# A cross-attention and FFN kernel: the token products first, the low-rank products second, those of the output weight behind the first quad

## The chip, the cores and the metric

One core of one Trainium2 chip. Times are device microseconds (us) of one execution. 1000 ns are 1 us. f32 is a 4-byte float; fp32r is the 4-byte form that TensorE multiplies in one pass; f32 takes it two.

## The reference

x is 64 sequences of 128 tokens, 256 wide. The context has 64 x 128 tokens of 192 channels; the last 4 of each sequence are separate context tokens with weights of their own.

```
q_in = xn @ Wq + xn @ q_down @ q_up * (alpha/32)          # xn = layernorm(x); Wq: 256 x 1024
k_in = org_ctx @ Wk + (the same with k_down, k_up)        # org_ctx: the first 124 tokens; Wk: 192 x 1024
v_in = org_ctx @ Wv + (the same with v_down, v_up)
out  = attention(q_in, k_in, v_in)                        # 16 heads of 64
out += attention(q_in, ipa_ctx @ Wk_ipa, ipa_ctx @ Wv_ipa)  # ipa_ctx: the last 4 tokens
x    = x + out @ Wo + bo + out @ o_down @ o_up * (alpha/32)
x    = x + ffn(layernorm(x))   # ternary weights w1, w2, a depthwise convolution over tokens, silu
```

The low-rank pairs have rank 32.

## The kernel before, in words

The five engines' instruction streams are written out by hand, each in one block (`block.sync`, `block.tensor`, `block.scalar`, `block.vector`, `block.gpsimd`), and wait for each other by semaphores. SP only issues transfers; so do ACT's first fourteen instructions. The work has two parts: a prologue that prepares the weights, and a loop over 16 groups of 4 sequences, in which each step of a group (`project`, `scores`, `p_v`, `finish` and the others) has a fixed place among 32 half steps, and steps of neighbouring groups are interleaved. The change touches the prologue alone.

In the prologue:

- `project(At(0), n)` for n below `EARLY_HALVES` = 10 loads x and the context of group 0, normalises x (POOL takes the power at L1008), transposes it (L394) and splits context and x into a high fp32r part (ACT, L606 to L611) and a low part (VectorE, L781 to L786).
- `lora_product(i)`, 12 times, multiplies down and up of a low-rank pair: 32 rows by 128 columns against 32 rows by 512, in f32, into one of five PSUM banks (L542). VectorE adds each product to the raw weight (a merge, L924). 4 products belong to Wq, 8 to Wk and Wv.
- Each raw weight of 128x1024 is then split: ACT writes the high part (`high_part`, L695), released by a count of merges (`du_of_split`), and VectorE the low part (`low_part`, L906). Numbers 0 and 1 are Wq's halves, 2 to 5 are WK, WV and the two remainders WKR and WVR, 6 and 7 the output weight's halves.
- The separate context tokens of all 64 sequences are multiplied by Wk_ipa (8 products of 2 matmuls with 96 rows and 256 columns, L558 and L559) and by Wv_ipa (4 products of 2 matmuls with 512 columns, L562 and L563). ACT copies the results (L704, L707), SP stores them to DRAM (L357, L358), from where each group loads its share; w1 and w2 are loaded into the same buffer when the stores have landed.
- `lora_product(i)` for i of 12 to 15 makes the output weight's low-rank product, 8 matmuls of 256 columns (L546), also with 32 rows.
- `project(At(0), n)` for n from 10 to 31 computes Q, K and V of three of the four quads of heads: for each quad two tiles of each, in the order Q0, K0, V0, Q1, K1, V1 (L405 six matmuls of 512 columns, L414 five, L424 ten of 256), which take turns in two PSUM banks. `N_V[1]` = 16 is the place of the first quad's V1. ACT copies Q (two copies into QM, L617 and L618), K (L623) and V1, VectorE copies V0 (L791).

The raw weights lie in buffers that the loop uses later: Wq, Wk and Wv and two of the up weights in QM, v_up and o_down in KT, the down weights in X2, the output weight in GBS, the token weights in V. So nothing may be copied to QM or KT before all raw weights in QM have been split; TensorE, ACT and POOL wait for that (`w_low`). POOL then zeroes half of QM (L1038, L1040), since each head pair is kept twice with one head's rows zero, and copies the token columns into KT (L1015).

The loads: SP issues x, context, Wq, Wk, Wv, the token weights and tokens, and Wo, in this order; ACT issues the alphas and the low-rank operands on its own queue.

Of the kernel before, what the change touches and what calls it, by code (L numbers as in the profile page):

```python
# [20 lines left out]
F32 = mybir.dt.float32  # L21
F32R = mybir.dt.float32r
BF16 = mybir.dt.bfloat16
ALU = mybir.AluOpType
# [3 lines left out]
P = 128  # L28
SEQS, TOK, DM = 64, 128, 256
CD = 192  # L30
CH = CD // 2
HEADS, DH = 16, 64
ID = HEADS * DH
RANK = 32
# [6 lines left out]
PAIRS = HEADS // 2  # L41
QUADS = HEADS // 4
CHUNKS = QUADS * NB
HALVES = 2 * CHUNKS
# [11 lines left out]
N_XT = 8  # L56
# [3 lines left out]
N_Q, N_K, N_V = (10, 14), (11, 15), (13, 16)  # L60
# [5 lines left out]
EARLY_HALVES = N_XT + 2  # L66
# [69 lines left out]
def program(nc, x, ctxT, cipaT, Wq, Wk, Wv, Wo, bo, q_downT, q_up, k_downT, k_up, v_downT, v_up, o_downT, o_up,  # L136
            alphas, Wk_ipa, Wv_ipa, w1T, conv_w, conv_b, w2T, out):
    with ExitStack() as ctx:
# [3 lines left out]
        def sem(name):  # L142
            return ctx.enter_context(nc.semaphore(name))
# [10 lines left out]
        BO = sb("BO", [P, DM])  # L154
# [66 lines left out]
        small_in = [sem(f"small_in{i}") for i in range(3)]  # L221
        w_in = [sem(f"w_in{i}") for i in range(5)]
        du_full, du_used = sem("du_full"), sem("du_used")
        wsum, wsum_all, wscale = sem("wsum"), sem("wsum_all"), sem("wscale")
        w_high, w_low = sem("w_high"), sem("w_low")
        wq_steps = sem("wq_steps")
# [71 lines left out]
        splits += [(wo_raw[:, 4 * k:4 * k + 4, :], WO[0][:, 4 * k:4 * k + 4, :], WO[1][:, 4 * k:4 * k + 4, :], 1.0) for k in range(2)]  # L298
        du_of_split = [2, 4, 7, 8, 11, 12, 14, 16]

        block = ctx.enter_context(nc.Block())
# [3 lines left out]
        def _(sp):  # L305
# [36 lines left out]

            for n in range(EARLY_HALVES):
                project(At(0), n)

            sp.dma_start(wq_raw, Wq.rearrange("(k p) n -> p k n", p=P)).then_inc(w_in[0], 16)
            for t, tr, src in ((wk_raw, wkr_raw, Wk), (wv_raw, wvr_raw, Wv)):
                sp.dma_start(t, src[0:P, :]).then_inc(w_in[1], 16)
                sp.dma_start(tr[0:64, :], src[P:CD, :]).then_inc(w_in[1], 16)
                sp.dma_start(tr[64:128, :], src[P:CD, :]).then_inc(w_in[1], 16)  # L350
            for t, tr, src in ((wki_raw, wkir_raw, Wk_ipa), (ci_t, cir_t, cipaT), (wvi_raw, wvir_raw, Wv_ipa)):
                sp.dma_start(t[0:CH, :], src[0:CH, :]).then_inc(w_in[4], 16)
                sp.dma_start(tr[0:CH, :], src[CH:CD, :]).then_inc(w_in[4], 16)
            sp.dma_start(wo_raw, Wo.rearrange("(k p) n -> p k n", p=P)).then_inc(w_in[2], 16)

            sp.wait_ge(kv_used, 12)
# [24 lines left out]
        def _(pe):  # L381
# [145 lines left out]
            pe.wait_ge(ident, 3)  # L527
            for n in range(EARLY_HALVES):
                project(At(0), n)

            def lora_product(i):
                need(pe, du_used, i - 4)
                if i == 0:
                    pe.wait_ge(small_in[0], 3 * 16)
                if i == 4:
                    pe.wait_ge(small_in[1], 6 * 16)
                if i == DU_O:
                    pe.wait_ge(small_in[2], 5 * 16)
                bank = PS[:, i % 5, :]
                if i < DU_O:  # L540
                    dn, k, up, c, _, _ = du[i]
                    mm(bank, dn[0:RANK, P * k:P * k + P], up[0:RANK, 512 * c:512 * c + 512], start=True, stop=True).then_inc(du_full, 1)  # L542
                else:
                    for a in range(2):
                        k = 2 * (i - DU_O) + a
                        m = mm(bank[:, DM * a:DM * a + DM], o_dn_t[0:RANK, P * k:P * k + P], o_up_t[0:RANK, :], start=True, stop=True)  # L546
                    m.then_inc(du_full, 1)

            for i in range(DU_O):
                lora_product(i)  # L550

            pe.wait_ge(w_in[4], 6 * 16)
            pe.wait_ge(du_used, DU_O)
            for i in range(12):
                need(pe, kv_used, i - 2)
                bank = PS[:, i % 3, :]
                if i < PAIRS:
                    mm(bank[:, 0:256], wki_raw[0:CH, P * i:P * i + P], ci_t[0:CH, :], start=True, stop=False)  # L558
                    mm(bank[:, 0:256], wkir_raw[0:CH, P * i:P * i + P], cir_t[0:CH, :], start=False, stop=True).then_inc(kv_full, 1)  # L559
                else:  # L560
                    a, c = divmod(i - PAIRS, 2)
                    mm(bank, ci_t[0:CH, P * a:P * a + P], wvi_raw[0:CH, 512 * c:512 * c + 512], start=True, stop=False)  # L562
                    mm(bank, cir_t[0:CH, P * a:P * a + P], wvir_raw[0:CH, 512 * c:512 * c + 512], start=False, stop=True).then_inc(kv_full, 1)  # L563
            pe.wait_ge(kv_used, 12)
            for i in range(DU_O, DU_N):
                lora_product(i)
            pe.wait_ge(w_low, 6)
            for n in range(EARLY_HALVES, HALVES):
                project(At(0), n)
            pe.wait_ge(zeroed, 2)  # L570
            pe.wait_ge(w_low, len(splits))

# [28 lines left out]
        def _(act):  # L601
# [76 lines left out]

            for t, src in ((SMALL[:, 0:4], alphas.broadcast_to([P, 4])), (q_dn_t[0:RANK, :], q_downT), (q_up_t[0:RANK, :], q_up)):
                act.dma_start(t, src).then_inc(small_in[0], 16)  # L680
            for t, src in ((k_dn_t[0:RANK, 0:CD], k_downT), (v_dn_t[0:RANK, 0:CD], v_downT),
                           (k_dn_t[0:RANK, CD:256], k_downT[:, P:CD]), (v_dn_t[0:RANK, CD:256], v_downT[:, P:CD]),
                           (k_up_t[0:RANK, :], k_up), (v_up_t[0:RANK, :], v_up)):
                act.dma_start(t, src).then_inc(small_in[1], 16)
            for t, src in ((o_dn_t[0:RANK, :], o_downT), (o_up_t[0:RANK, :], o_up),
                           (BO[:], bo.broadcast_to([P, DM])), (CW[:], conv_w), (CB[:], conv_b)):
                act.dma_start(t, src).then_inc(small_in[2], 16)
            for n in range(EARLY_HALVES):
                project(At(0), n)

            def high_part(i):

                raw, high, _, factor = splits[i]
                act.wait_ge(du_used, du_of_split[i])
                act.activation(high, raw, ACT.Identity, scale=factor).then_inc(w_high, 1)  # L695

            for i in range(6):
                high_part(i)

            for i in range(12):  # L700
                act.wait_ge(kv_full, i + 1)
                bank = PS[:, i % 3, :]
                if i < PAIRS:
                    act.activation(ki_all[:, :, i, :], bank[:, 0:256].rearrange("p (g n) -> p g n", g=GROUPS), ACT.Identity).then_inc(kv_used, 1)  # L704
                else:
                    a, c = divmod(i - PAIRS, 2)
                    act.activation(vi_t[:, a, 512 * c:512 * c + 512], bank, ACT.Identity).then_inc(kv_used, 1)  # L707
            for i in range(6, len(splits)):
                high_part(i)
            act.wait_ge(w_low, 6)  # L710
            act.wait_ge(du_used, DU_N)
            for n in range(EARLY_HALVES, HALVES):
                project(At(0), n)
            act.wait_ge(small_in[2], 5 * 16)

# [19 lines left out]
        def _(dve):  # L735
# [164 lines left out]
            dve.wait_ge(w_in[0], 16)  # L900
            low = 0

# [5 lines left out]

            for i in range(DU_N):
                dve.wait_ge(du_full, i + 1)  # L910
                bank = PS[:, i % 5, :]
                if i == 4:
                    dve.wait_ge(w_in[1], 6 * 16)
                if i == DU_O:
                    while low < 6:
                        low_part(low)
                        low += 1
                    dve.wait_ge(w_in[2], 16)
                if i < DU_O:
                    raw, k = du[i][4], du[i][5]  # L920
                else:
                    a = 2 * (i - DU_O)
                    raw, k, bank = wo_raw[:, a:a + 2, :], 3, bank.rearrange("p (a n) -> p a n", a=2)
                dve.scalar_tensor_tensor(out=raw, in0=bank, scalar=SMALL[:, k:k + 1], in1=raw,  # L924
                                         op0=ALU.mult, op1=ALU.add).then_inc(du_used, 1)
                while low < 6 and du_of_split[low] + 3 <= i:
                    low_part(low)
                    low += 1
            dve.wait_ge(kv_used, 12)
            for i in range(6, len(splits)):  # L930
                low_part(i)
            for n in range(EARLY_HALVES, HALVES):
                project(At(0), n)


# [55 lines left out]
        def _(pool):  # L991
# [4 lines left out]
            pool.wait_ge(ident, 2)  # L996
            pool.tensor_copy(IDB[:], IDF[:]).then_inc(ident, 1)
            pool.wait_ge(consts, 1)

# [35 lines left out]

            pool.wait_ge(w_low, 6)
            pool.wait_ge(du_used, DU_O)
# [68 lines left out]
```

## Time and profile before

| | us |
|---|---|
| median of 3 runs | 1582.96 (1582.52 to 1586.33) |
| the profiled execution | 1581.49 |
| its span, first to last instruction | 1579.7 |
| busy in it: TensorE, VectorE, ScalarE, GpSimd | 1447.4, 1218.0, 1178.2, 648.4 |
| first score products start | 84.9 |

PE is TensorE's matmul side, PEld its weight loads, DVE VectorE, ACT ScalarE, POOL GpSimd, SP SyncE; a q behind a name is that engine's sequencer, where transfers are issued. An operation is named by its line (L542), by what it writes and what it reads, and by its shape, partitions x elements. PEclk is the granted clock of TensorE as a share of 2.4 GHz. "[0.55 <-ACT QM L618]" behind a row means that the engine stood idle for 0.55 us and that this instruction of ACT ended it. A row that holds several instructions (x16) gives the time from the first's start to the last's end.

### The profile page before, as it was taken

How to read it: one execution, taken by the hardware profiler on the slowest of the kernel's cores; microseconds unless marked ns; L12 is line 12 of the kernel's file. 1: busy time of each engine (PE TensorE's matmuls, PEld its weight loads, DVE VectorE, ACT ScalarE, POOL GpSimd, SP SyncE). 2: the span in 40 equal slices, each digit the busy share in tenths (PEclk: the TensorE clock that was granted, in tenths of full speed). 3: DMA queues.
4: the chain of work that ended last, by engine and by line, in shares of the span. 5: the costliest groups of instructions: out<-in, count | busy, mean ns of one | idle time of the engine just before them, and what ended most of it. 6: DMA issues, size and time to landing. Idle time of an engine off the chain costs nothing.

```text
span 1579.7 us, 33324 instructions
## 1 busy us (share of the span) xinstructions
PE 1447.4 (92%) x10732; PEld 1178.4 (75%) x10778; DVE 1218.0 (77%) x3061; ACT 1178.2 (75%) x3909; POOL 648.4 (41%) x1053
## 2 busy tenths in 40 slices
PE   6999999999999999999999999999999999999742
PEld 3778878787787878787787878778787878777521
DVE  4254688787969888787978878787987879686966
ACT  2477896978878797887879697887879788786721
POOL 0134443544444344444444354444434444444500
PEclk9899999999999999999999999999999999999965
DMA  7400001000010100000010000001010000000000
GB/s 198 123 30 16 30 16 30 16 28 29 14 42 14 42 0 27 29 27 29 14 42 14 29 14 27 29 14 42 14 42 0 27 29 27 29 1 28 1 14 13
DMA packets 41128, 47.13 MB, mean 30 GB/s; under 512 B 3008, under 2 KB 35200, under 8 KB 41088
## 3 DMA queue, kind: packets, MB, share of 16 engines
q1 hardware_dynamic: 40032, 45.82, 9.4%
q10 hardware_dynamic: 1056, 0.81, 0.2%
q8 instruction: 22, 0.36, 0.1%
q14 instruction: 18, 0.15, 0.0%
HBM read 36.13 MB, written 10.49 MB: 30 GB/s over the span
## 4 chain that ended last, share of the span: by engine, by line
PE 52%; ACT 19%; DVE 18%; issue 9%; DMA 0%; DVEq 0%; POOL 0%; ACTq 0%; POOLq 0%
PE PS L462 10%; ACT SM L650 8%; PE PS L424 7%; PE PS L475 6%; PE PS L405 5%; PE PS L440 5%; PE PS L449 4%; PE PS L414 4%; PE PS L523 3%; ACT HP L671 2%; DVE GBS L865 2%; PE PS L502 2%; DVE GBS L886 2%; ACT GBS L676 2%; ACT QM L617 1%
## 5 line engine op out<-in xcount | busy, mean ns | idle before, releaser
L1025 POOL TENSOR_TENSOR SM<-SM,RC 128x496 f32<-128x496 f32 (+1 forms) x512 | 331.6, 668 | 748.6 <-DVE RC L800 748.6
L650 ACT ACTIVATE SM<-PS,MX 128x124 f32<-128x124 f32 x1024 | 358.7, 365 | 147.1 <-DVE SM L806 145.0
L462 PE MATMUL PS<-KT,QM 128*128 128x128 f32 x2048 | 277.4, 278 | 29.6 <-ACT SM L650 29.4
L462 PEld LDWEIGHTS PS<-KT,QM 128*128 128x128 f32 x2048 | 248.8, 192 | 45.2 <-ACT SM L650 44.5
L650 ACT ACTIVATION_READ_ACCUMULATOR SM<-PS,MX 128x1 f32 x1024 | 212.7, 208 | 0.0
L1051 POOL TENSOR_TENSOR OTl<-OF,OTh 128x256 fp32r<-128x256 f32 x256 | 196.6, 768 | 14.5 <-ACT OF L644 14.5
L642 ACT ACTIVATE OTh<-PS 128x256 fp32r<-128x256 f32 x256 | 100.3, 392 | 116.1 <-PE PS L440 114.9
L449 PE MATMUL PS<-IDF,SM 128*128 128x128 f32 x1024 | 168.4, 287 | 8.2 <-POOL SM L1025 8.1
L804 DVE TENSOR_REDUCE MX<-PS 128x4 f32<-128x496 f32 x256 | 170.2, 665 | 0.0
L440 PE MATMUL PS<-PT,V 128*64 128x128 f32 x2048 | 168.8, 286 | 0.1
L440 PEld LDWEIGHTS PS<-PT,V 128*64 128x64 f32 x2048 | 106.8, 136 | 82.0 <-issue 75.0
L636 ACT ACTIVATE PT<-PS 128x512 f32<-128x512 f32 x256 | 157.0, 613 | 0.4 <-PE PS L449 0.4
L449 PEld LDWEIGHTS PS<-IDF,SM 128*128 128x128 f32 x1024 | 107.7, 141 | 54.4 <-issue 37.9
L803 DVE TENSOR_REDUCE MX<-PS 128x4 f32<-128x16 f32 x256 | 41.3, 161 | 124.7 <-PE PS L462 124.6
L865 DVE TENSOR_TENSOR GBS<-PS,BC 128x512 f32<-128x512 f32 x128 | 87.5, 684 | 60.8 <-PE PS L502 59.3
L671 ACT ACTIVATE HP<-GBS,CB,CW 128x512 f32<-128x512 f32 x128 | 111.3, 869 | 28.9 <-DVE GBS L865 27.5
L870 DVE SCALAR_TENSOR_TENSOR HP<-GBS,HP 128x512 f32<-128x512 f32 x128 | 110.4, 862 | 21.6 <-ACT GBS L676 20.9
L475 PE MATMUL PS<-WOh,OTh 128*128 128x256 f32 x512 | 123.6, 322 | 0.0
L850 DVE SCALAR_TENSOR_TENSOR HP<-GBS,CW,HP 128x508 f32<-128x508 f32 x128 | 119.2, 931 | 0.0
L856 DVE SCALAR_TENSOR_TENSOR HP<-GBS,CW,HP 128x508 f32<-128x508 f32 x128 | 103.8, 811 | 17.7 <-ACT HP L671 13.8
L405 PE MATMUL PS<-XTh,WQh 128*128 128x512 f32 x256 | 106.9, 417 | 0.0
L502 PE MATMUL PS<-Q1T,W 128*128 128x512 bf16 x210 | 70.8, 402 | 37.4 <-DVE GBS L865 28.8
(139 smaller groups left out, 3576.4 us busy)
## 6 DMA issues: line engine op xcount, KB each, us to landing
XIN<-in_x SPq DMA_DIRECT2D x16, 512.0 KB, 3.6
XRES<-in_x SPq DMA_DIRECT2D x16, 512.0 KB, 3.5
out_y<-HP SPq DMA_DIRECT2D x16, 512.0 KB, 3.0
CRAW<-in_ctxT SPq DMA_DIRECT2D x16, 256.0 KB, 2.7
RRAW<-in_ctxT SPq DMA_DIRECT2D x32, 128.0 KB, 2.8
QM<-in_Wq SPq DMA_DIRECT2D x1, 1024.0 KB, 11.0
GBS<-in_Wo SPq DMA_DIRECT2D x1, 1024.0 KB, 21.1
k_ipa_columns<-HP SPq DMA_DIRECT2D x1, 1024.0 KB, 5.1
```

The costliest lines, as they stand in the source:

```text
L405: m = mm(bank, WQ[w][:, k, P * tile:P * tile + P], XT[xt][:, k, :], start=(i == 0), stop=(i == 5))
L440: m = mm(psO[r:r + DH, h // 2, :], V[:, b, DH * (4 * q + h):DH * (4 * q + h) + DH], PT[:, h, :], start=True, stop=True)
L449: m = pe.transpose(psT[:, h, :], SM[c % 2][:, h, :], IDF[:])
L462: m = mm(psS[:, h, :], QM[:, 2 * q + h // 2, h % 2, TOK * b:TOK * b + TOK], KT[:, 2 * q + h // 2, b, :], start=True, stop=True)
L475: m = mm(psY[b // 2][:, b % 2, :], OT[ot][c % 2][:, a, :], WO[w][:, 2 * q + a, :], start=(q == 0 and i == 0 and b % 2 == 0), stop=(q == QU ...
L636: act.activation(PT[:], psT, ACT.Identity).then_inc(pt_done, 1)
L650: m = act.activation(SM[s % 2][:, h, 0:ORG], psS[:, h, 0:ORG], ACT.Exp, bias=MX[s % 2][:, h:h + 1], accum_out=SU[s % 2][:, h:h + 1])
L671: act.activation(HT[j].rearrange("p (b t) -> p b t", b=NB), GB[j % 4], ACT.Identity, bias=CB[:, j:j + 1], scale=CW[:, j, 1:2]).then_inc(t1 ...
L804: dve.tensor_reduce(MX[s % 2][:, 0:4], psS[:, :, 0:ORG], AX.X, ALU.max, negate=True)
L850: dve.scalar_tensor_tensor(out=y[:, :, 0:TOK - 1], in0=GB[j % 4][:, :, 1:TOK], scalar=CW[:, j, 2:3], in1=y[:, :, 0:TOK - 1], op0=ALU.mult, ...
L1025: m = pool.tensor_tensor(part, part, RC[c % 2][:, 4 * i:4 * i + 4].unsqueeze(2).broadcast_to(shape), ALU.mult)
L1051: pool.tensor_tensor(OT[1][c % 2][:], OF[:], OT[0][c % 2][:].bitcast(F32), ALU.subtract).then_inc(ot_done, 1)
```

## The change

The four prologue streams are reordered.

- SP loads the token weights of K and the tokens right behind x, those of V behind the context, then Wq, Wk and Wv; the fourteen small loads that ACT issued now stand in SP's queue, nine of them ahead of Wo and five behind, and all wait for three new memsets of POOL.
- TensorE computes the token products of K first, then transposes x, then the token products of V, then the 12 low-rank products, then Q0, K0 and so on; the output weight's low-rank products follow V1 of the first quad.
- The low-rank matmuls read all 128 partitions of their operands instead of 32; the other 96 were zeroed by POOL's memsets.
- The low parts of WV and WVR (3 and 5) move from VectorE to POOL, with a semaphore of their own, `wv_low`.
- The merges, high and low parts of the output weight move to `LORA_O + 1` = 17 in the projection steps of ACT and VectorE.

```
# SP
 project(At(0), 0)
 ipa_weights(wki_raw, wkir_raw, Wk_ipa, 4)
 ipa_weights(ci_t, cir_t, cipaT, 4)
 for n in range(1, EARLY_HALVES):
     project(At(0), n)
 ipa_weights(wvi_raw, wvir_raw, Wv_ipa, 5)
 (Wq, Wk, Wv as before)
+sp.wait_ge(padded, 3)
+(small_in[0]: 3 loads, small_in[1]: 6 loads)
 (Wo)
+(small_in[2]: 5 loads)
# TensorE
-mm(bank, dn[0:RANK, P * k:P * k + P], up[0:RANK, 512 * c:512 * c + 512], start=True, stop=True)
+mm(bank, dn[:, P * k:P * k + P], up[:, 512 * c:512 * c + 512], start=True, stop=True)
...
+pe.wait_ge(w_in[4], 4 * 16)
+for i in range(PAIRS):
+    ipa_product(i)
+for n in range(EARLY_HALVES):
+    project(At(0), n)
+pe.wait_ge(w_in[5], 2 * 16)
+for i in range(PAIRS, 12):
+    ipa_product(i)
 pe.wait_ge(kv_used, 12)
+for i in range(DU_O):
     lora_product(i)
+pe.wait_ge(w_low, 2)
+for n in range(EARLY_HALVES, HALVES):
+    if n == FIRST_K:
+        pe.wait_ge(w_low, 4)
+    if n == FIRST_V:
+        pe.wait_ge(wv_low, 2)
+    project(At(0), n)
+    if n == LORA_O:
+        for i in range(DU_O, DU_N):
+            lora_product(i)
# ScalarE
+for n in range(N_XT):
+    project(At(0), n)
+for i in range(PAIRS):
+    ipa_copy(i)
+for n in range(N_XT, EARLY_HALVES):
+    project(At(0), n)
+for i in range(PAIRS, 12):
+    ipa_copy(i)
+for i in range(6):
+    high_part(i)
+act.wait_ge(w_low, 4)
+act.wait_ge(wv_low, 2)
 for n in range(EARLY_HALVES, HALVES):
     project(At(0), n)
+    if n == LORA_O + 1:
+        high_part(6)
+        high_part(7)
# VectorE
+for i in range(DU_O):
+    if i == 4:
+        dve.wait_ge(w_in[1], 6 * 16)
+    merge(i)
+    if i == 5:
+        low_part(0)
+    if i == 7:
+        low_part(1)
+low_part(2)
+low_part(4)
 for n in range(EARLY_HALVES, HALVES):
     project(At(0), n)
+    if n == LORA_O + 1:
+        dve.wait_ge(w_in[2], 16)
+        for i in range(DU_O, DU_N):
+            merge(i)
+        low_part(6)
+        low_part(7)
# GpSimd
+pool.memset(x2_flat, 0.0).then_inc(padded, 1)
+pool.memset(qm_flat[:, 6144:8192], 0.0).then_inc(padded, 1)
+pool.memset(kt_flat[:, 2048:4096], 0.0).then_inc(padded, 1)
...
+for i in (3, 5):
+    raw, high, lo_, _ = splits[i]
+    pool.wait_ge(w_high, i + 1)
+    pool.tensor_tensor(lo_, raw, high.bitcast(F32), ALU.subtract).then_inc(wv_low, 1)
+pool.wait_ge(w_low, 4)
+pool.wait_ge(wv_low, 2)
 pool.memset(QM[0:64, :, 1, :], 0.0).then_inc(zeroed, 1)
```

## Rows read from the trace of the kernel before

**Rows 1.** The page, part 1: busy us (share of the span), instructions.
```profile
PE 1447.4 (92%) x10732; PEld 1178.4 (75%) x10778; DVE 1218.0 (77%) x3061; ACT 1178.2 (75%) x3909; POOL 648.4 (41%) x1053
```
**Rows 2.** Busy us by stage: PE, PEld, DVE, ACT, POOL; PEclk; DMA share; GB/s.
```profile
2.00:9.00 7.00, 0.00 (x0) 0.00 (x0) 1.95 (x10) 0.00 (x0) 0.46 (x1) 1.00 0.87 232
9.00:25.00 16.00, 13.87 (x22) 6.38 (x23) 9.34 (x16) 5.74 (x7) 0.56 (x1) 1.00 1.05 280
39.50:53.10 13.60, 12.91 (x44) 8.01 (x44) 0.07 (x1) 4.69 (x10) 0.00 (x0) 1.00 0.02 5
53.20:63.40 10.20, 10.20 (x27) 7.64 (x26) 7.28 (x8) 3.87 (x5) 7.01 (x2) 0.50 0.76 255
86.50:88.20 1.70, 0.70 (x4) 0.22 (x2) 1.50 (x6) 1.48 (x10) 0.00 (x0) 1.00 0.00 0
85.00:1474.00 1389.00, 1324.76 (x10202) 1098.35 (x10244) 1111.36 (x2853) 1112.09 (x3768) 622.73 (x1016) 1.00 0.08 24
```
**Rows 3.** The chain of waits, 13 to 85 us: start us, us, what.
```profile
13.07 19.08 PE PS L542 x22
...
34.87 1.19 PE PS L558 x2
...
38.62 0.85 PE PS L558 x2
...
40.00 0.43 PE PS L558 x2
...
44.32 0.86 PE PS L562 x2
...
51.87 5.93 PE PS L546 x16
57.80 2.86 PE PS L405 x6
...
62.79 1.52 PE PS L424 x10
...
66.34 0.60 ACT QM L618
...
66.99 1.44 PE PS L424 x10
...
71.12 1.45 PE PS L424 x10
...
84.92 0.91 PE PS L462 x8
```
**Rows 4.** The timeline: start us, us, engine, line, operation.
```profile
10.79 1.01 SPq L354 DMA_DIRECT2D GBS<-in_Wo  x1
...
17.60 1.06 ACT L695 ACTIVATE WQh<-QM 128x1024 fp32r<-128x1024 f32 x1 [3.90 <-DVE QM L924]
...
24.31 1.22 DVE L906 SCALAR_TENSOR_TENSOR WQl<-QM,WQh 128x1024 fp32r<-128x1024 f32 x1
...
55.31 2.06 DVE L924 SCALAR_TENSOR_TENSOR GBS<-PS,SMALL,GBS 128x512 f32<-128x512 f32 x3
55.45 3.50 POOL L1038 MEMSET QM<- 64x4096 f32 x1 [45.89 <-DVE WVRl L906]
...
102.62 1.03 PE L394 MATMUL PS<-IDF,XIN 128*128 128x128 f32 x8
...
104.26 0.69 DVE L782 TENSOR_TENSOR CTR<-RRAW,CTR 64x512 fp32r<-64x512 f32 x1
104.28 1.26 POOL L1051 TENSOR_TENSOR OTl<-OF,OTh 128x256 fp32r<-128x256 f32 x1
...
107.81 0.74 POOL L1051 TENSOR_TENSOR OTl<-OF,OTh 128x256 fp32r<-128x256 f32 x1
```
**Rows 5.** POOL's groups by line and shape: xcount, busy us, mean ns, idle before.
```profile
L1025 POOL TENSOR_TENSOR SM<-SM,RC 128x496 f32<-128x496 f32 x256 | 259.5, 1014 | 748.6 <-DVE RC L800 748.6
```
**Rows 6.** DMA issues: count, KB each, us from issue to landing.
```profile
KT<-in_v_up ACTq DMA_DIRECT2D x1, 128.0 KB, 7.9
```

More of the change, by code:

```diff
@@ L221, in program @@
         small_in = [sem(f"small_in{i}") for i in range(3)]
-        w_in = [sem(f"w_in{i}") for i in range(5)]
+        w_in = [sem(f"w_in{i}") for i in range(6)]
         du_full, du_used = sem("du_full"), sem("du_used")
         wsum, wsum_all, wscale = sem("wsum"), sem("wsum_all"), sem("wscale")
-        w_high, w_low = sem("w_high"), sem("w_low")
+        w_high, w_low, wv_low = sem("w_high"), sem("w_low"), sem("wv_low")
+        padded = sem("padded")
         wq_steps = sem("wq_steps")
@@ L299, in program @@
         du_of_split = [2, 4, 7, 8, 11, 12, 14, 16]
+        LORA_O, FIRST_K, FIRST_V = N_V[1], N_K[0], N_V[0]
         block = ctx.enter_context(nc.Block())
@@ L341, in finish, with ipa_weights @@
                     sp.dma_start(seqs(out, g), OUTT).then_inc(out_done, 16)
-            for n in range(EARLY_HALVES):
+            def ipa_weights(t, tr, src, i):
+                sp.dma_start(t[0:CH, :], src[0:CH, :]).then_inc(w_in[i], 16)
+                sp.dma_start(tr[0:CH, :], src[CH:CD, :]).then_inc(w_in[i], 16)
+            project(At(0), 0)
+            ipa_weights(wki_raw, wkir_raw, Wk_ipa, 4)
+            ipa_weights(ci_t, cir_t, cipaT, 4)
+            for n in range(1, EARLY_HALVES):
                 project(At(0), n)
+            ipa_weights(wvi_raw, wvir_raw, Wv_ipa, 5)
             sp.dma_start(wq_raw, Wq.rearrange("(k p) n -> p k n", p=P)).then_inc(w_in[0], 16)
@@ L350, in _ @@
                 sp.dma_start(tr[64:128, :], src[P:CD, :]).then_inc(w_in[1], 16)
-            for t, tr, src in ((wki_raw, wkir_raw, Wk_ipa), (ci_t, cir_t, cipaT), (wvi_raw, wvir_raw, Wv_ipa)):
-                sp.dma_start(t[0:CH, :], src[0:CH, :]).then_inc(w_in[4], 16)
-                sp.dma_start(tr[0:CH, :], src[CH:CD, :]).then_inc(w_in[4], 16)
+            sp.wait_ge(padded, 3)
+            for t, src in ((SMALL[:, 0:4], alphas.broadcast_to([P, 4])), (q_dn_t[0:RANK, :], q_downT), (q_up_t[0:RANK, :], q_up)):
+                sp.dma_start(t, src).then_inc(small_in[0], 16)
+            for t, src in ((k_dn_t[0:RANK, 0:CD], k_downT), (v_dn_t[0:RANK, 0:CD], v_downT),
+                           (k_dn_t[0:RANK, CD:256], k_downT[:, P:CD]), (v_dn_t[0:RANK, CD:256], v_downT[:, P:CD]),
+                           (k_up_t[0:RANK, :], k_up), (v_up_t[0:RANK, :], v_up)):
+                sp.dma_start(t, src).then_inc(small_in[1], 16)
             sp.dma_start(wo_raw, Wo.rearrange("(k p) n -> p k n", p=P)).then_inc(w_in[2], 16)
+            for t, src in ((o_dn_t[0:RANK, :], o_downT), (o_up_t[0:RANK, :], o_up),
+                           (BO[:], bo.broadcast_to([P, DM])), (CW[:], conv_w), (CB[:], conv_b)):
+                sp.dma_start(t, src).then_inc(small_in[2], 16)
             sp.wait_ge(kv_used, 12)
@@ L527, in _ @@
             pe.wait_ge(ident, 3)
-            for n in range(EARLY_HALVES):
-                project(At(0), n)
             def lora_product(i):
@@ L541, in lora_product @@
                     dn, k, up, c, _, _ = du[i]
-                    mm(bank, dn[0:RANK, P * k:P * k + P], up[0:RANK, 512 * c:512 * c + 512], start=True, stop=True).then_inc(du_full, 1)
+                    mm(bank, dn[:, P * k:P * k + P], up[:, 512 * c:512 * c + 512], start=True, stop=True).then_inc(du_full, 1)
                 else:
@@ L545, in lora_product, with ipa_product @@
                         k = 2 * (i - DU_O) + a
-                        m = mm(bank[:, DM * a:DM * a + DM], o_dn_t[0:RANK, P * k:P * k + P], o_up_t[0:RANK, :], start=True, stop=True)
+                        m = mm(bank[:, DM * a:DM * a + DM], o_dn_t[:, P * k:P * k + P], o_up_t[:], start=True, stop=True)
                     m.then_inc(du_full, 1)
[L549 to L554, printed above, removed]
+            def ipa_product(i):
                 need(pe, kv_used, i - 2)
@@ L563, in _ @@
                     mm(bank, cir_t[0:CH, P * a:P * a + P], wvir_raw[0:CH, 512 * c:512 * c + 512], start=False, stop=True).then_inc(kv_full, 1)
+            pe.wait_ge(w_in[4], 4 * 16)
[6 more added lines that the diff above has]
+                ipa_product(i)
             pe.wait_ge(kv_used, 12)
-            for i in range(DU_O, DU_N):
+            for i in range(DU_O):
                 lora_product(i)
+            pe.wait_ge(w_low, 2)
[8 more added lines that the diff above has]
+                        lora_product(i)
+            pe.wait_ge(zeroed, 2)
             pe.wait_ge(w_low, 6)
[L568 to L571, printed above, removed]
             def ternary(g, n):
@@ L677, in finish @@
                                    scale=0.5).then_inc(th_done, 1)
[L679 to L689, printed above, removed]
             def high_part(i):
@@ L695, in high_part, with ipa_copy @@
                 act.activation(high, raw, ACT.Identity, scale=factor).then_inc(w_high, 1)
-            for i in range(6):
-                high_part(i)
-            for i in range(12):
+            def ipa_copy(i):
                 act.wait_ge(kv_full, i + 1)
@@ L707, in _ @@
                     act.activation(vi_t[:, a, 512 * c:512 * c + 512], bank, ACT.Identity).then_inc(kv_used, 1)
-            for i in range(6, len(splits)):
+            for n in range(N_XT):
[7 more added lines that the diff above has]
+            for i in range(6):
                 high_part(i)
-            act.wait_ge(w_low, 6)
-            act.wait_ge(du_used, DU_N)
+            act.wait_ge(w_low, 4)
+            act.wait_ge(wv_low, 2)
             for n in range(EARLY_HALVES, HALVES):
                 project(At(0), n)
+                if n == LORA_O + 1:
+                    high_part(6)
+                    high_part(7)
             act.wait_ge(small_in[2], 5 * 16)
@@ L900, in _ @@
             dve.wait_ge(w_in[0], 16)
-            low = 0
             def low_part(i):
@@ L907, in low_part, with merge @@
                                          op0=ALU.mult, op1=ALU.subtract).then_inc(w_low, 1)
-            for i in range(DU_N):
+            def merge(i):
                 dve.wait_ge(du_full, i + 1)
                 bank = PS[:, i % 5, :]
[L912 to L918, printed above, removed]
                 if i < DU_O:
@@ L925, in _ @@
                                          op0=ALU.mult, op1=ALU.add).then_inc(du_used, 1)
[L926 to L931, printed above, removed]
+            for i in range(DU_O):
[8 more added lines that the diff above has]
+            low_part(4)
             for n in range(EARLY_HALVES, HALVES):
                 project(At(0), n)
+                if n == LORA_O + 1:
[4 more added lines that the diff above has]
+                    low_part(7)
             raws = ((w1_raw, W1), (w2_raw, W2))
@@ L1034, in _ @@
                 project(At(0), n)
-            pool.wait_ge(w_low, 6)
+            for i in (3, 5):
[4 more added lines that the diff above has]
+            pool.wait_ge(wv_low, 2)
             pool.wait_ge(du_used, DU_O)
```

## The prediction

> **What bounds the kernel now.** I read the page first: TensorE is busy 92% of the span [rows 1]. Then the busy time by stage [rows 2]: from 85 us on TensorE is busy for 1324.8 of 1389 us, at full clock. The change touches nothing of that loop, so what it can earn lies in the 85 us ahead of the first score products. There the chain of waits [rows 3] names what ends last: the low-rank products (L542, 19.08 us), the token products (L558 to L563, 34.87 to about 51.2), the low-rank products of the output weight (L546, 5.93), then the projections of three quads, until the scores start at 84.92. The reader is to see that nearly all of it is TensorE, and not transfers.
>
> The same rows tell what a product costs. An f32 product is two passes. L542's 22 passes of 512 columns take 0.87 us each; L562's two take 0.86 together, 0.43 each. So one of them runs at half the pace of the other: 1.2 against 2.4 GHz. L558 shows the step, 0.85 a product at 38.62 and 0.43 at 40.00. The granted clock reads 1.00 from 39.5 to 53.1 and 0.50 from 53.2 to 63.4 [rows 2]; ahead of 39.5 the pace is what tells the level. So 19 us of products with 32 rows never raised the clock, 4.6 us of products with 96 rows did, and it fell 1.3 us after the 32-row products of L546 had begun. The prologue is a question of this clock.
>
> **The change part by part.** I lay the new order out in time.
>
> *Transfers.* 0.232 MB/us moved from 2 to 9 us (1.62 MB), 0.28 from then on [rows 2]. The token weights of K and the tokens now stand behind x: 0.52 + 0.79 + 0.20 = 1.51 MB, moved at 8.6, seen at about 9.2. Then in the new order, summed: context 2.03 MB, token weights of V 2.82, Wq, Wk and Wv 5.96, q's low-rank operands 6.13, k's and v's 6.46, Wo 7.5. At 0.28 the 6.13 are there at 25.1 and the 6.46 at 26.3. Fourteen issues move from ACT's queue to SP's. Wo, SP's 18th issue, began at 10.79 [rows 4], 0.6 each, so the nine small ones are issued by about 16.5, ahead of their turn. SP's new wait for three memsets holds back those nine, Wo and the last five; 64x4096 took 3.50 us [rows 4], so 5120 columns take POOL 4.4, from about 2 to 6.5, and SP comes there at 10.8. Cost none, nor if the memsets were nearly twice as long.
>
> *Token products of K.* The same work from 9.2. They took from 34.87 to 44.32 with the clock rising within [rows 3]; again 9.45: 18.65. Transposes of x 1.03 at full clock [rows 4]: 19.7. ACT's copies of context and x run beside the token products of V, which take 6.88 (8 matmuls of 0.86), with their banks free: 26.6, plus the last copy and its way back, 0.67 (51.2 to 51.87): 27.3.
>
> *Low-rank products*, from 27.3, as q's operands have landed. TensorE now reads 128 rows, 96 of them zero. Bounds for one product: 0.86 us (L562, 96 rows at full clock) and 1.73 (two passes of L542). I take 0.86, by the nearer row: more rows than there, and the engine comes from 17 us of unbroken work. VectorE then sets the pace. Its first six merges follow the products, 28.4 to 33.4; then a low part (1.15 of its 1.22 us before the next can start), two merges (0.70 each), a low part, four merges: 39.9. ScalarE's high parts (1.06) five and six, released by merges 11 and 12, end at 40.3 and 41.4; VectorE's last two low parts at 41.1 and 42.3 [rows 4].
>
> *POOL's two low parts* are new, 128x1024 with two operands. Bounds: 1.5 us, by extending the step from 256 columns (0.74) to 496 (1.01), and 3.0, four times the 256 [rows 4, 5]. I take 2.1, in proportion to the 496, the nearest in size. The second needs high part six, 41.4, and by itself ends at 43.5. But L1051 took 1.26 us with VectorE's L782 (both inputs in SBUF) under its first 0.67, and 0.74 without [rows 4], so I let it wait for VectorE's last low part: 42.3 + 2.1 = 44.4.
>
> The Trainium skill (SBUF — State Buffer, on VectorE with two SBUF inputs against GpSimd) states that whichever starts later is blocked for the whole of the other's instruction. The trace agrees: 0.52 of 0.69 us lost. With that rule the sum has 0.9 us more than without.
>
> Behind ACT's wait for this low part stand all its copies into QM and K. Behind TensorE's stands V0. Behind POOL's stand two memsets of 3.5 us and the K columns; these end by 53 and have time until the scores. Q0 (37.8 to 39.2) and K0 (42.3 to 43.5) have run meanwhile, but both banks are full until ACT's two QM copies, 0.60 each [rows 3]: V0 starts at 45.7, which was 62.79.
>
> TensorE has 2.6 us of work between 37.8 and 45.7, 1.2 of it behind 39.2. The clock fell before in a denser stretch, so I take it as fallen at V0 and back some 5 us later (4.6 at L558, 5.6 from L405's start at 57.80). At 1.2 GHz V0 takes 2.13 and Q1 2.56 (L405 took 2.86 with its start), then come the copies and K1: V1 6.4 us after V0, where it took 4.20 (62.79 to 66.99). V1 from 52.1 to 53.5.
>
> *The output weight's products* stand there now: 16 passes at 0.215, L558's pace at 40.00, are 3.45 us, where they took 5.93: 57.0. Q of the second quad ends 58.4. ACT's high part stands before its QM copy: last product 57.1, merge 57.8, high part 58.9, copies 60.1; V at 60.2, which was 71.12. From there 13.80 us to the scores as before [rows 3]: 74.0 against 84.92. VectorE's two low parts end at about 60 and hold up nothing.
>
> **Sum**: 10.9 us less. The profiled execution took 1581.49 us, 1.8 beyond its span of 1579.7, and lies 1.5 below the median of 1582.96. It should come to 1570.6, and the median to 1582.96 - 10.9 = 1572.1. Nothing in the loop gives back an earlier start: TensorE bounds it at 95%, and the DMA engines are at 8% [rows 2].
>
> **The rivals.**
>
> *Clock held through the gap.* V1 follows V0 by 3.9 instead of 6.4: 1569.6. For: between 86.5 and 88.2 TensorE was busy for 0.70 of 1.70 us and kept its clock [rows 2]. Against: the gap here is four times as long. The Trainium skill (TensorE: Matmul & The Clock Gate, in its closing table) also warns of idle gaps between bursts of matmuls. Chance 0.08.
>
> *Zero rows don't count.* The clock falls some 1.3 us into the low-rank products, as at L546. 10.5 of 12 products then cost 1.73: last one 46.8, last merge 47.6, POOL's low part 51.5, V0 52.8, 7.1 later than forecast. The output weight's products add 2.5 and the Q behind them 0.5: 10.1 of the 10.9 are gone, 1582.2. For: no row has a product with most rows zero. Against: half of QM's rows are zero in every score product, and the loop keeps its clock [rows 2]. Chance 0.14.
>
> *The small transfers come late.* They had a queue of their own and the engines from the start; now they stand behind 5.96 MB. If they land 8 us late, the low-rank products start at 33.1, 5.8 later: 1577.9. For: the order. Against: 0.28 MB/us were kept from 9 to 25 us, mostly by SP's queue alone [rows 2]. Chance 0.09.
>
> *Slower.* v_up, the last of ACT's first nine transfers, landed 7.9 us after its issue [rows 6]; nine in a row at 0.88 us each would be that. If 32-row transfers on one queue don't overlap, and behind the big ones cost 2 us each, the last lands at 43, 16 later than 27.3, and the kernel is 5 us slower: 1588. It decides from 1.5 us each on. Against: those 7.9 us were shared with x, context and Wq, so alone they need less. Chance 0.05.
>
> That leaves 0.64 for the forecast. Its own range is 1568.5 to 1575.5: POOL's bounds (0.6 down, 0.9 up), the landing at 9.2 (0.7 down, 1.5 up), and the moment of the clock's rise (1.7 both ways at the first products, and again behind V0).
>
> **How the numbers follow.** 0.3% (4.7 us) is about what can be told here from no change. Faster than 1578.2: 0.64 + 0.08 + somewhat over half of the late transfers: 0.77. Within 0.3%: the zero rows and the rest of the late transfers: 0.18. Slower: 0.05. The range holds the forecast, the held clock and most of the late transfers, and leaves out the centre of the zero rows and the slower case: 1566.5 to 1580.5.
>
> **What would show it.** The first token product at 9 to 10 us; passes of 0.43 us in the low-rank products; last merge near 40; POOL's second low part ending near 44.4, V0 right behind ACT's copies; a clock of 0.50 somewhere between 43 and 52 us; the output weight's products in 3.4 to 3.5 us; scores near 74.0. Passes of 0.85 in the low-rank products would make the forecast wrong, and so would low-rank products that start behind 31 us because a landing is late.

## The result, and the profile after

| | before | after |
|---|---|---|
| median, us | 1582.74 (1582.16 to 1586.33, 4 runs) | 1571.08 (1568.71 to 1572.11, 4 runs) |
| ratio | | 0.9916, 95% interval 0.9902 to 0.9931 |
| span of the profiled execution | 1579.7 | 1569.0 |
| first score products | 84.92 | 72.19 |

The forecast was 1572.1. The chain of waits of the kernel after, in the rows that answer to [rows 3] (start us, us, what; L567 to L572 are the token products, L556 and L560 the low-rank products, L421, L430 and L440 the projections Q, K and V, L642 and L643 the QM copies, L478 the scores):

```profile
8.30 1.19 PE PS L567 x2
...
12.57 0.43 PE PS L568 x2
...
17.32 0.88 PE PS L410 x8
18.19 0.86 PE PS L571 x2
...
25.10 0.61 ACT HP L717
...
25.75 5.43 PE PS L556 x12
...
35.54 2.64 DVE QM L938 x4
38.17 1.17 DVE WKl L927
39.35 1.15 DVE WKRl L927
40.49 2.31 issue
42.80 0.59 ACT QM L642
43.40 0.60 ACT QM L643
...
44.14 2.48 PE PS L440 x10
46.61 2.56 PE PS L421 x6
49.17 1.44 PE PS L430 x5
50.61 1.29 PE PS L440 x10
51.90 3.47 PE PS L560 x16
...
58.37 1.44 PE PS L440 x10
...
72.19 0.91 PE PS L478 x8
```

The reader is to see three things. The low-rank products go at 0.45 us a pass, where [rows 3] had 0.87. From the last merge (38.17) to V0 (44.14) TensorE is not on the chain: the low parts and what is called "issue" here set it. And V0 and Q1 take 2.48 and 2.56, where experiment 3 has 1.41 and 1.42 at full clock. The "issue" of 2.31 us is ACT waiting for POOL's low part, as the timeline shows (start us, us, engine, line, operation):

```profile
35.87 2.39 POOL L1067 TENSOR_TENSOR WVl<-QM,WVh 128x1024 fp32r<-128x1024 f32 x1 [28.18 <-ACT WVh L708]
39.27 1.21 DVE L927 SCALAR_TENSOR_TENSOR WKRl<-QM,WKRh 128x1024 fp32r<-128x1024 f32 x1
39.64 3.08 POOL L1067 TENSOR_TENSOR WVRl<-QM,WVRh 128x1024 fp32r<-128x1024 f32 x1 [1.37 <-ACT WVRh L708]
42.80 0.59 ACT L642 ACTIVATE QM<-PS 64x512 f32<-64x512 f32 x1 [3.24 <-issue]
```

And busy time by stage (columns as in [rows 2]) has the clock at 0.50 for the stretch in which V0 and Q1 lie. It fell at 42.8, within TensorE's wait for V0, and was back at 49.6, within K1:

```profile
12.10:42.80 30.70, 26.35 (x83) 14.58 (x82) 15.87 (x21) 13.22 (x22) 5.47 (x2) 1.00 1.01 305
42.80:49.60 6.80, 5.46 (x18) 4.82 (x19) 0.69 (x1) 2.15 (x4) 6.72 (x2) 0.50 0.43 64
49.70:72.10 22.40, 21.58 (x115) 17.43 (x115) 6.78 (x8) 11.55 (x19) 2.92 (x7) 1.00 0.00 1
```

The scores start 12.73 us earlier; the span ends 10.7 earlier. The loop keeps nearly all of the lead: the last sum of its exponentials is read out at 1486.41 against 1498.79, 12.38 ahead. The rest, 1.7 us, is lost in the drain, the work of the last group behind that point. First before, then after, the stage from there to the end:

```profile
1498.80:1579.70 80.90, 31.87 (x159) 19.61 (x160) 54.49 (x112) 18.32 (x31) 4.38 (x6) 0.62 0.04 13
```
```profile
1486.40:1569.00 82.60, 33.51 (x160) 19.99 (x160) 54.48 (x112) 18.31 (x31) 4.36 (x6) 0.60 0.04 13
```

VectorE and ScalarE have the same busy time in both, TensorE 1.6 us more at a lower mean clock. This is one execution of each. Over the ten profiled executions of this document, each of another kernel, the drain took 80.2 (experiment 8) to 82.8 us (experiment 1), in no order that follows the length of the prologue. By the medians the gain is 11.7 us, 1.0 more than between the two profiled executions. So a loss of 1.7 us in the drain is what this pair shows, and not shown to be the change's doing.

### The profile page after: what moved, and what is told of

The parts are those of the page before. It is cut to its first block, busy times and chain, and to the rows that moved or that the text cites. A ratio compares the mean times of both kernels' runs of the same rounds, so it can differ in the third digit from the quotient of the medians.

```text
span 1569.0 us, 33374 instructions
## 1 busy us (share of the span) xinstructions
PE 1441.2 (92%) x10778; PEld 1174.6 (75%) x10778; DVE 1214.9 (77%) x3059; ACT 1177.5 (75%) x3909; POOL 660.0 (42%) x1058
## 4 chain that ended last, share of the span: by engine, by line
PE 52%; ACT 20%; DVE 19%; issue 9%; DMA 0%; DVEq 0%; ACTq 0%; POOL 0%; SPq 0%; POOLq 0%
PE PS L478 10%; ACT SM L675 8%; PE PS L440 8%; PE PS L491 6%; PE PS L421 5%; PE PS L456 5%; PE PS L465 4%; PE PS L430 4%; PE PS L539 4%; ACT HP L696 2%; DVE GBS L887 2%; PE PS L518 2%; DVE GBS L908 2%; ACT GBS L701 2%; ACT QM L642 2%
## 5 line engine op out<-in xcount | busy, mean ns | idle before, releaser
L478 PE MATMUL PS<-KT,QM 128*128 128x128 f32 x2048 | 278.2, 279 | 29.3 <-ACT SM L675 29.2
L478 PEld LDWEIGHTS PS<-KT,QM 128*128 128x128 f32 x2048 | 249.4, 192 | 44.8 <-ACT SM L675 44.5
L696 ACT ACTIVATE HP<-GBS,CB,CW 128x512 f32<-128x512 f32 x128 | 111.3, 870 | 28.7 <-DVE GBS L887 27.3
L518 PE MATMUL PS<-Q1T,W 128*128 128x512 bf16 x256 | 81.4, 401 | 31.5 <-DVE GBS L887 28.7
L421 PE MATMUL PS<-XTh,WQh 128*128 128x512 f32 x256 | 107.3, 419 | 0.0
```

The costliest lines, as they stand in the source:

```text
L421: m = mm(bank, WQ[w][:, k, P * tile:P * tile + P], XT[xt][:, k, :], start=(i == 0), stop=(i == 5))
L478: m = mm(psS[:, h, :], QM[:, 2 * q + h // 2, h % 2, TOK * b:TOK * b + TOK], KT[:, 2 * q + h // 2, b, :], start=True, stop=True)
L696: act.activation(HT[j].rearrange("p (b t) -> p b t", b=NB), GB[j % 4], ACT.Identity, bias=CB[:, j:j + 1], scale=CW[:, j, 1:2]).then_inc(t1 ...
```

## Experiments

Eight kernels in two groups, 1 to 4 and 5 to 8; each group had its own runs of the kernel before beside it (medians 1582.69 and 1583.27), and ratios are to those. The kernel after has 0.9916 against its own runs of the kernel before (1582.74). Where two intervals overlap, the times alone don't tell the two kernels apart; "scores" is of one execution each. "Scores" is the start of the first score products, from the chain of waits.

| kernel | median us | ratio, 95% interval | scores |
|---|---|---|---|
| after | 1571.08 | 0.9916 [0.9902, 0.9931] | 72.19 |
| 1 order without padding | 1578.35 | 0.9962 [0.9948, 0.9976] | 78.52 |
| 2 padding without order | 1577.85 | 0.9969 [0.9954, 0.9984] | 76.31 |
| 3 gap filled | 1568.73 | 0.9902 [0.9886, 0.9919] | 70.24 |
| 4 output weight's products in the gap | 1566.89 | 0.9889 [0.9872, 0.9905] | 68.58 |
| 5 low part on VectorE | 1568.58 | 0.9909 [0.9895, 0.9923] | 71.61 |
| 6 combined | 1560.53 | 0.9867 [0.9852, 0.9882] | 64.16 |
| 7 small loads on ACT's queue | 1576.53 | 0.9963 [0.9949, 0.9976] | 78.05 |
| 8 combined, warmed | 1560.67 | 0.9872 [0.9854, 0.9890] | 62.16 |

### 1. The new order without the padding

```
-mm(bank, dn[:, P * k:P * k + P], up[:, 512 * c:512 * c + 512], ...)
+mm(bank, dn[0:RANK, P * k:P * k + P], up[0:RANK, 512 * c:512 * c + 512], ...)
```
(and so for the output weight's. Everything else of the change stays: the order, the queues, the memsets, POOL's low parts.)

> The changed kernel, but the low-rank matmuls read 32 rows again; order, queues and memsets stay. Theory (128 rows, zero or not, are what holds the clock): TensorE comes from the token products at 2.4 GHz, the clock falls 1 to 5 us into the low-rank products, some 9 of 12 then cost 1.71 us, V0 starts near 51 instead of 44.1 and the first scores at 80 to 82.5 instead of 72.2; the kernel at 1578.5 to 1581. Rival (the order alone does it: an engine that comes warm stays warm): passes of 0.43 us throughout, scores at 72.2, 1571.

The theory held. The low-rank products began at 26.0 at full pace; the clock fell at 29.8, and the last of them ended near 43. Timeline of TensorE, then the stages:

```profile
26.00 5.17 PE L556 MATMUL PS<-QM,X 32*128 32x512 f32 x10 [0.69 <-ACT HP L717]
30.97 1.91 PE L556 MATMUL PS<-KT,X 32*128 32x512 f32 x2
```
```profile
12.80:29.70 16.90, 16.21 (x55) 9.46 (x55) 5.09 (x8) 7.60 (x15) 0.00 (x0) 1.00 1.07 298
29.80:46.80 17.00, 16.75 (x23) 6.97 (x22) 11.04 (x13) 5.35 (x6) 4.07 (x2) 0.50 0.87 261
```

From 26.0 to 43.0 TensorE had no gap, in 32-row products alone, and from 29.8 on it was at half clock. In the kernel after, the same products with 128 rows addressed kept it. So TensorE's busy time doesn't explain the fall; the rows do. The padding is worth 6.3 us of scores in this order. The scores came at 78.52, earlier than the expected 80 to 82.5, as the clock was back from 46.8 to 50. It fell twice more: behind a wait of 1.9 us before V0, and at 60.6, as the 32-row products of the output weight ended; the Q behind them took 2.85 us instead of 1.42.

### 2. The padding without the order

```
 # before.py
+pool.memset(x2_flat, 0.0) ... (three memsets), and ACT waits for them ahead of its loads
-mm(bank, dn[0:RANK, ...], up[0:RANK, ...], ...)
+mm(bank, dn[:, ...], up[:, ...], ...)
```

> The kernel before in its old order, but the low-rank matmuls read 128 rows (zeroed by three memsets, for which ACT's small loads wait). Theory (rows hold and also raise the clock): the low-rank products start 1 to 3 us later as their loads do, rise to 2.4 GHz after 3 to 7 us, the token products run at full clock from the start, the output weight's take 3.45 us and the clock is not lost at L546; scores near 75 to 78 instead of 84.9, the kernel at 1573 to 1576. Rival (order is what counts, and zeros hold a clock but can't raise it): the low-rank products stay at 0.85 us a pass, scores at 83 to 86, the kernel at 1581 to 1584.

```profile
15.20 6.83 PE L543 MATMUL PS<-QM,X 128*128 128x512 f32 x10 [4.23 <-DMA QM<-in_q_up]
21.87 1.02 PE L543 MATMUL PS<-KT,X 128*128 128x512 f32 x2
...
31.19 0.67 PE L559 MATMUL PS<-SM,V 96*128 96x256 f32 x2 [3.14 <-DVE QM L926]
```

Ten passes in 6.83 us, then 0.43 each: the pace doubled at about 19.7, 4.5 us into products of which three quarters are zeros. Zeros raised the clock here as they held it in the kernel after; that settles the "zero rows don't count" rival, of which the trace before had said nothing. The padding has a price: the products start at 15.20 instead of 13.07, as ACT's loads wait for the memsets until 6.2. TensorE then waits 3.14 us for the merges, and the token products behind that wait still go at 0.43 a product from the second on: this wait did not cost the clock. The scores came at 76.31, as the theory had it. The median is 1577.85, 2 us above what was expected; its seven runs spread from 1574.9 to 1580.31, and the profiled one, at the lower end with 1575.03, is the only one whose prologue can be read.

Together, in the profiled executions: the padding alone brings 8.6 us of scores, the rest of the change (experiment 1) 6.4, both 12.7, which is 2.3 less than the sum. By the medians it is 4.8, 4.3 and 11.7, which is 2.5 more than the sum. So each of the two is worth several us, and whether they overlap stays open. How many rows are enough, and whether those of the loaded weights or those of the moving operand count, was not tried.

### 3. The gap filled with work of no use

```
 if n == FIRST_K:
+    for _ in range(12):
+        mm(psF, XT[0][:, 0, 0:P], XT[0][:, 0, :], start=True, stop=True)
     pe.wait_ge(w_low, 4)
 if n == FIRST_V:
+    (8 of the same)
     pe.wait_ge(wv_low, 2)
```

> The changed kernel with 12 matmuls of no use (fp32r, 128x512, into the bank that the FFN uses later) between Q0 and K0 and 8 between K0 and V0, where TensorE waits. Theory (the gap costs the clock, and the clock costs 2.4 us there): clock 1.00 throughout from about 12 us, V0 in 1.2 instead of 2.48 us, V1 at 4.0 behind V0 instead of 6.47, scores near 69.8 instead of 72.2, the kernel 2.4 us faster than the changed one: about 1568.7. Rival (ACT's copies set the pace behind V0, so the clock is free there): scores within 0.5 of 72.2, 1571. A second rival: fp32r work of this kind does not hold it and the clock falls at the same place.

```profile
44.42 1.41 PE PS L440 x10
45.83 1.42 PE PS L421 x6
...
48.52 1.44 PE PS L440 x10
```
```profile
12.70:44.40 31.70, 30.57 (x102) 18.04 (x101) 15.89 (x21) 14.13 (x23) 6.81 (x3) 1.00 1.01 290
44.40:70.20 25.80, 24.85 (x133) 20.25 (x134) 7.47 (x9) 12.53 (x20) 8.46 (x8) 1.00 0.05 14
```

The clock stays, V1 follows V0 by 4.10 us instead of 6.47, and from V0 to the scores it takes 25.82 instead of 28.05. The median is 2.35 us lower, but the intervals of the two ratios overlap, so it is the trace that shows it: twenty matmuls of no use pay for themselves.

### 4. The gap filled with work that has to be done

```
-if n == LORA_O:
+if n == N_Q[0]:
     for i in range(DU_O, DU_N):
         lora_product(i)
```

> The changed kernel with the output weight's low-rank products right behind Q0 (in the gap before K0) instead of behind V1; merges and splits of the output weight stay where they are. Theory: TensorE's 3.47 us behind V1 leave the path, the gap is filled and the clock held (2.4 us); ACT's two high parts in front of its QM copy give back 1.2: scores at 67 to 68, 4.5 to 5 us less than the changed kernel, about 1566.5. Rival (the clock falls anyway in the 1.8 us before V0): scores near 70. Rival (K0 comes later and the time is given back in front of V0): scores at 71 to 72.

The token products of K took 10.3 us here, as the clock rose at 14.8 instead of 12.1, so all is 1.4 us later up to V0 (45.55). From there to the scores it is 23.03 us against 28.05, 5.0 less, as expected. The scores themselves, 68.58, are 3.6 earlier and miss the expected 67 to 68 by those 1.4 us. ACT's high parts are on the chain, also as expected:

```profile
51.12 0.60 ACT V L654
51.73 1.89 ACT WOh L708 x2
53.62 0.48 ACT QM L642
```

### 5. POOL's second low part on VectorE

```
 low_part(2)
 low_part(4)
+low_part(5)
...
-for i in (3, 5):
+for i in (3,):
```
(TensorE, ACT and POOL wait for five of VectorE's low parts and one of POOL's instead.)

> The changed kernel with the low part of WVR (number 5) on VectorE behind its two others; POOL keeps number 3. Theory (POOL's second low part, which started under VectorE's last and took 3.08 us, sets when ACT's first QM copy and V0 start): the low part ends at 41.6 instead of 42.7, V0 starts 1.1 us earlier, scores at 71.1 instead of 72.2, the kernel 1 us faster than the changed one (1570). Rival (the split in two engines is what makes V0 early): VectorE's extra 1.15 us delays everything behind it, scores at 72.2 or later.

Low-rank products to V0: 26.81 to 44.10, 17.29 us, against 25.75 to 44.14, 18.39: 1.1 less, as expected. To the scores 44.80 against 46.44, 1.6 less. The low part ended at 42.7, the same time as in the kernel after, only because the prologue had run 1.06 us behind by then. What ends last in front of V0 is now K0, as the chain of waits shows:

```profile
41.60 2.50 PE PS L430 x5
```

The clock fell at 41.1 here, within the wait of 2.83 us before K0; in the kernel after it outlived a wait of the same length (2.82) and fell in the next. ACT's QM copies ended at 43.9, just ahead of K0, so the two are nearly level. The medians differ by 2.5 us, but they come from two groups of runs, and their ratios (0.9909 and 0.9916) can't be told apart.

### 6. All of it

```
# TensorE: as in 4; VectorE and POOL: as in 5
# ScalarE
-act.wait_ge(w_low, 4)
-act.wait_ge(wv_low, 2)
+act.wait_ge(w_low, 2)
 for n in range(EARLY_HALVES, HALVES):
+    if n == N_QUAD[1] + N_Q[0]:
+        act.wait_ge(w_low, 5)
+        act.wait_ge(wv_low, 1)
     project(At(0), n)
-    if n == LORA_O + 1:
+    if n == N_QUAD[1] + N_K[0] + 1:
         high_part(6)
         high_part(7)
# VectorE: merges of the output weight at N_V[0] + 1, its low parts at N_QUAD[1] + N_V[0] + 1
```

> Four edits in one: output weight's products in the gap behind Q0; low part 5 on VectorE; ACT waits only for Wq's splits before it copies the first quad's Q (tiles 0 and 1 of QM lie on Wq's raw halves) and for the others in front of the second quad; merges of the output weight right behind V0's copy, its high and low parts in the second quad, where ACT has 2 us between copies. Theory (each of these was on the path): V0 starts behind K0 at 42 to 43.5 instead of 44.1, clock held, no wait of Q's copy for high parts, scores at 64 to 66, 6 to 8 us less than the changed kernel: about 1564. Rival (the parts overlap in what they save, as K0 now ends later): scores at 67.5 to 68.5 as with the products' move alone, 1566.9.

```profile
25.71 10.57 PE PS L556 x24
36.28 1.39 PE PS L421 x6
37.66 3.45 PE PS L560 x16
41.12 1.16 PE PS L430 x5
42.28 1.18 PE PS L440 x10
43.46 1.41 PE PS L421 x6
...
46.14 1.43 PE PS L440 x10
```

TensorE is on the chain without a break from 25.71 to 44.9, all of it at full clock. From the start of the low-rank products to the scores it takes 38.45 us, 8.0 less than after. The median is 1560.53, 10.6 below the kernel after and 22.7 below the kernel before of its group. Between the two profiled executions the span is 10.8 us shorter: 8.0 ahead of the scores, 0.5 in the loop, and 2.3 in the drain, which took 80.3 us here with a mean clock of 0.64. The last part need not be the change's doing, as said above. No version has a lower median.

### 7. The small loads back on ACT's queue

```
-sp.wait_ge(padded, 3), and the fourteen loads on sp
+act.wait_ge(padded, 3), and the fourteen loads on act, ahead of its first project step
```

> The changed kernel with the fourteen small loads back on ACT's queue, behind the three memsets. Theory (the queue and the place of the small loads matter only by what they take from the first landings): the tokens' landing at 8.2 moves by less than 0.5, the low-rank products start with the last token copy as now, scores within 0.7 of 72.2, the kernel within 1 us of 1571. Rival (they were moved for bandwidth): from 6.5 us on they take their share from x, the token weights and the context, the first token product starts 1 us or more later, and all behind it.

Neither held. The first token product still started at 8.21, so nothing was lost to bandwidth; but the kernel is 5.5 us slower than after. ACT issues its loads itself, here from 6.25 on, when the last memset had ended, and until the last is out it copies nothing (timeline; the last row is from the chain of waits):

```profile
6.25 0.39 ACTq L711 DMA_DIRECT2D SMALL<-in_alphas  x1
...
13.03 0.45 ACTq L718 DMA_DIRECT2D CB<-in_conv_b  x1
13.52 1.28 ACT L704 ACT_TABLE_LOAD   x1 [13.52 <-issue]
14.81 0.94 ACT L704 ACTIVATE HP<-PS 128x256 f32<-128x256 f32 x3
15.25 1.22 PE PS L557 x2
```

ACT's first copy of a token product starts at 14.81, against 10.39 after. TensorE has three banks for these products and stands still until 15.25; the low-rank products start at 31.49 instead of 25.75. In the kernel before, ACT issued the same fourteen loads from 0.74 on, without a wait, and this was its first work behind them:

```profile
10.35 0.63 ACT L606 ACTIVATE CTh<-CRAW 128x512 fp32r<-128x512 f32 x1
```

That is no later than the 10.39 of the kernel after. So the issues alone would have been out in time: what makes them late here is the wait for the memsets in front of them. This is argued from the two traces; the new order with ACT's issues and without that wait was not run.

### 8. The clock raised before the first load

```
+for _ in range(15):
+    mm(psF[:, 0:P], IDF[:], IDF[:], start=True, stop=True)
 pe.wait_ge(w_in[4], 4 * 16)
```

(On top of experiment 6.)

> The combined kernel with 15 f32 matmuls of the identity by itself (128 columns, of no use) before the first token product, while TensorE waits for the load. Theory (what comes before decides the clock, whatever the data): the clock rises at 5 to 8 us instead of 12 to 15, the eight token products of K take 6.9 us instead of 9.0 to 10.3, the low-rank products start when q's operands are there at 23.8 to 24.5 instead of 25.8 to 27.2, scores 1.5 to 3 us before those of the combined kernel, and its runs spread less. Rival (a matmul of 128 columns on mostly zeros doesn't count): as the combined kernel. A second: the matmuls run past the landing at 8.2 and cost what they overrun.

```profile
1.89 5.93 PE L575 MATMUL PS<-IDF 128*128 128x128 f32 x30 [1.89 <-POOL IDB L1029]
8.02 0.70 PE L567 MATMUL PS<-SM,V 96*128 96x256 f32 x2 [0.19 <-DMA SM<-in_cipaT]
8.55 0.59 PE L568 MATMUL PS<-SM,V 96*128 96x256 f32 x2
```

In the profiled run the mechanism is there: full pace from 8.5 us, the low-rank products at 23.75, bound by the landing of q_up at 23.6, and the scores at 62.16, 2.0 before those of 6. That run took 1558.01. But the median of four runs, 1560.67, is that of 6, and the runs spread more (1558.01 to 1565.17), not less. Whether the others failed to rise in time or lost it again in the drain stays open.

## Why the prediction was right

Its mechanism held step by step. That the profiled execution came out so near (1570.99 measured, 1570.6 forecast) is in part luck, as two errors of size cancelled in it; the median (1571.08) is 1.0 below the forecast of 1572.1.

**The clock and the padding.** Forecast: passes of 0.43 us in the low-rank products, since 128 addressed rows hold the clock. Measured 0.43 to 0.45. It was the largest single assumption, argued from the nearer row; experiments 1 and 2 show it: with 32 rows the clock falls on an engine that is busy all the time, with 96 rows of zeros it even rises. The last merge came 12.4 us behind the start of the products, forecast 12.6.

**Landings.** Forecast 9.2 for the first token product, measured 8.30: from 2 to 9 us 292 GB/s were moved, where the forecast had taken 232 from the kernel before; why it is more was not tried. q's operands were there by 23.77 (forecast 25.1), ahead of need, so the late-transfers rival and the slower one had nothing to stand on.

**Token products and transposes.** 9.02 and 0.88 us against 9.45 and 1.03; the low-rank products started at 25.75 against 27.3. This 1.55 is nearly all by which the forecast missed the scores (74.0 against 72.19): 0.90 of it is the landing, 0.43 the token products, 0.15 the transposes. Only the 0.43 is a matter of when the clock rises: experiment 4 has 10.3 for the same products.

**POOL's low parts.** Forecast 2.1 us and a wait for VectorE, ending at 44.4, which was 17.1 behind the start of the low-rank products. Measured 2.39 for the free one, 3.08 for the one that started 0.84 us before VectorE's low part ended at 40.48, end 42.72: 17.0 behind. 40.48 + 2.39 is 42.87, so the wait was nearly whole; experiments 3, 4 and 7 have 3.07 to 3.10 for the same instruction. By the Trainium skill (SBUF — State Buffer, "SBUF: two separate sides"), whichever starts later is blocked for the other's whole instruction. The trace comes near to that: 0.69 of 0.84 us were lost here.

**The gap.** Forecast: the clock falls there, V1 6.4 us behind V0. Measured: 0.50 from 42.8 to 49.6, V1 6.47 behind. V0 itself took 2.48 for 2.13, and K1, by then partly at full clock, 1.44. Experiment 3 prices the fall: 2.23 us to the scores. It came with two waits, 2.8 us before K0 and 2.2 before V0, and the 1.4 us of K0 between them did not prevent it. The Trainium skill's warning of idle gaps (TensorE: Matmul & The Clock Gate, closing table) agrees with this trace. The length of a wait alone doesn't tell, though: experiment 2 kept the clock through 3.14 us, experiment 5 lost it in 2.83.

**The output weight's products.** 3.45 forecast, 3.47 measured. From their end to V of the second quad, with ACT's high part before its QM copy, 3.0 us against 3.2 worked out, and from there to the scores 13.82 against 13.80.

**The step that was off** is the last: "Nothing in the loop gives back an earlier start". The loop gave back 0.35 us, and the drain behind it, which the forecast took as unchanged, was 82.6 us instead of 80.9 in the two profiled executions, with a lower mean clock. So 12.7 us at the scores became 10.7 at the end of the span, and the forecast of 10.9 came out near it with 1.8 too little at one end and 2.1 too much at the other. By the medians the gain is 11.7, so part of that loss belongs to the executions that were profiled. That the drain's length is the clock's doing is argued from the two rows above and not shown; why the clock fell differently there was not tried.

**What the prediction did not see.** It priced the move of the small loads to SP at nothing. As a cost that is so; but undone it costs 5.9 us of scores (experiment 7), because ACT's issues, which now wait for the memsets, stand ahead of ACT's copies.

## What to carry to other kernels

Read TensorE's clock from the spacing of equal passes, and give it full rows: a product with 32 rows was no slower by itself (0.43 us a pass in experiment 1 until the clock fell), but a stretch of them cost the clock, and zeroed rows held and raised it. Zeroing has to end before the loads that share the buffer, so see which engine waits for it. When a wait on TensorE can't be removed, put work into it that must be done anyway; here the same four products cost 3.5 us behind V1 and nothing in the gap, and kept the clock besides. Count a transfer's issue against the engine that issues it, and ask what that engine has to do next.

## What the runs showed of the hardware that I had not expected

- 32-row f32 products back to back ran at half clock from 29.8 to 43.0 us, with TensorE busy all the time (experiment 1); the same products with 96 zero rows raised it after 4.5 us (experiment 2).
- A wait of 3.14 us left the clock up (experiment 2), one of 2.83 us did not (experiment 5: it fell at 41.1, 2.3 us behind the last matmul), and one of 2.82 us did, but not the next of 2.18 (after).
- The moment at which the pace of the token products doubled differed between executions of the same work: 12.1, 12.2, 12.7, 12.7, 13.8 and 14.8 us (after and experiments 6, 3, 1, 5, 4), for a first product at 8.1 to 8.8. That alone moves the prologue by up to 1.4 us, and with the drain (80.2 to 82.8 us) it is as large as the spread of most kernels' runs.
